# One batched banded-attention kernel: each engine branches on its own, and three loads change their place on SyncE's queue

## The reference

```python
x = x + 0.5 * _L0_ffn_ref(_layernorm(x), gate_w, w1, b1, w2, b2)
x = x + _L0_attn_ref(_layernorm(x), Wq, Wk, Wv, Wo)
x = x + 0.5 * _L0_ffn_ref(_layernorm(x), gate_w, w1, b1, w2, b2)
```

## Time and profile before

| | us |
|---|---|
| median of 3 runs (lowest to highest) | 862.96 (862.14 to 865.73) |
| the profiled execution | 860.79 |
| its span, first to last instruction | 858.7 |
| PE busy in it | 811.9 (95%) |
| DVE, ACT, POOL busy | 743.2, 634.7, 481.3 |
| mean granted TensorE clock | 0.994 of full |

### The profile page before, as it was taken

How to read it: one execution, slowest core, us unless ns; L and a number is a source line. 1 busy time by engine, 2 the same in 40 slices (tenths; PEclk the granted TensorE clock), 3 DMA queues, 4 the chain that set the end, 5 groups by cost and what they waited for, 6 DMA issues and landing times.

```text
span 858.7 us, 50541 instructions
## 1 busy us (share of the span) xinstructions
PE 811.9 (95%) x21504; PEld 611.7 (71%) x21505; DVE 743.2 (87%) x2788; ACT 634.7 (74%) x1418; POOL 481.3 (56%) x856
## 2 busy tenths in 40 slices
PE   9798999999999999999999999899999999999795
PEld 8555666777777777667778778667777777766573
DVE  7898899998987899998888799998988789999663
ACT  2268878997877667898777676899777767788760
POOL 3212556675554566766555466766555465766661
PEclk9999999999999999999999999999999999999899
DMA  7722224332212335442222234533222244321212
GB/s 230 119 83 69 68 77 131 106 106 68 87 52 92 114 105 165 117 123 68 81 74 74 95 126 144 148 103 92 69 71 67 92 126 127 102 75 35 78 43 90
DMA packets 93195, 83.55 MB, mean 97 GB/s; under 512 B 17568, under 2 KB 92192, under 8 KB 92960
## 3 DMA queue, kind: packets, MB, share of 16 engines
q1 hardware_dynamic: 91360, 78.91, 30.3%
q10 hardware_dynamic: 1600, 1.31, 1.0%
HBM read 20.66 MB, written 8.39 MB: 34 GB/s over the span
## 4 chain that ended last, share of the span: by engine, by line
PE 67%; DVE 13%; ACT 9%; issue 4%; SPq 2%; DMA 2%; POOL 1%; ACTq 0%; DVEq 0%
PE bank L1093 14%; PE bank L1075 11%; PE bank L1041 11%; PE bank L930 10%; PE bank L945 6%; PE bank L913 6%; DVE bank L1485 6%; ACT probs L1218 4%; PE bank L1113 3%; PE bank L899 2%; DVE stats L698 1%; SPq L830 1%; ACT xn L1131 1%; PE bank L866 1%; DVE row_max L1485 1%
## 5 line engine op out<-in xcount | busy, mean ns | idle before, releaser
L1218 ACT ACTIVATE probs<-bank 128x384 f32<-128x384 f32 (+1 forms) x1024 | 460.0, 481 | 143.3 <-PE bank L1075 125.2
L1485 DVE CUSTOM_DVE_ANT_0 bank<-bank,con 128x288 f32<-128x288 f32 x1024 | 494.3, 519 | 52.7 <-PE bank L1041 44.4
L1041 PE MATMUL bank<-k_stack,q_stack 96*32 96x288 bf16 x4096 | 325.2, 288 | 9.7 <-DVE row_max L1485 5.1
L1075 PE MATMUL bank<-q_stack,k_stack 99*32 99x288 bf16 (+3 forms) x4096 | 320.3, 286 | 11.4 <-ACT probs L1218 8.3
L1093 PE MATMUL bank<-probs,v_sb 128*32 128x128 f32 x5888 | 307.6, 273 | 6.0 <-issue 4.8
L1287 POOL TENSOR_SCALAR_AFFINE_SELECT probs<-probs 128x512 f32<-128x512 f32 x240 | 154.7, 644 | 179.9 <-ACT probs L1218 179.4
L1093 PEld LDWEIGHTS bank<-probs,v_sb 128*32 128x32 f32 x5888 | 194.2, 111 | 38.4 <-issue 8.2
L1041 PEld LDWEIGHTS bank<-k_stack,q_stack 96*32 96x32 bf16 x4096 | 126.6, 95 | 72.5 <-DVE row_max L1485 21.0
L1075 PEld LDWEIGHTS bank<-q_stack,k_stack 99*32 99x32 bf16 x4096 | 125.2, 95 | 69.2 <-ACT probs L1218 44.3
L1292 POOL TENSOR_SCALAR_AFFINE_SELECT probs<-probs 128x512 f32<-128x512 f32 x240 | 153.6, 640 | 17.0 <-ACT probs L1218 16.9
L930 PE MATMUL bank<-xnT,wqk_sb 128*32 128x256 f32 x2048 | 157.7, 379 | 0.6 <-DVE neg_max L1507 0.5
(11 more groups left out here) (123 smaller groups left out, 718.9 us busy)
## 6 DMA issues: line engine op xcount, KB each, us to landing
q_stack<-pieces SPq DMA_DIRECT2D x384, 64.0 KB, 2.7
k_stack<-pieces SPq DMA_DIRECT2D x364, 64.0 KB, 2.7
x_ring<-in_x SPq DMA_DIRECT2D x28, 512.0 KB, 4.8
out_x<-x_ring SPq DMA_DIRECT2D x16, 512.0 KB, 4.3
attn<-in_x SPq DMA_DIRECT2D x4, 512.0 KB, 6.1
wback_sb<-in_wback SPq DMA_DIRECT2D x8, 256.0 KB, 5.8
k_stack<-pieces ACTq DMA_DIRECT2D x20, 64.0 KB, 3.5
q_stack<-neg_max SPq DMA_DIRECT2D x48, 16.0 KB, 2.3
```

Source lines behind the costliest of these rows:

```text
L1041: last = pe.matmul(a_ring[i % len(a_ring)][SP * s:SP * (s + 1), 0:WIN], q_stack[g % 2][0:KROWS, h, q:q + SP], k_stack[g % 2][0:KROWS, h, q ...
L1075: last = pe.matmul(score_bank(i)[SP * s:SP * (s + 1), start:final], k_stack[g % 2][0:SROWS, h, WINDOW + P * j + SP * s:WINDOW + P * j + SP ...
L1218: act.activation(probs[:, j % 4, h, c0:c1], score_bank(i)[:, c0:c1], ACT.Exp, scale=LOGIT_SCALE).then_inc(S["exp_ready"], 1)
L1485: dve.tensor_tensor_reduce(out=a_ring[i % len(a_ring)][:, 0:WIN], in0=a_ring[i % len(a_ring)][:, 0:WIN], in1=mask, scale=1.0, scalar=con[: ...
```

## The change

In four parts:

1. The first `attend` has no Block any more. Its five functions are called one after the other with the engines, so no barrier stands at its end.
2. Every engine waits for `found` >= 2 (the flag is written), loads the flag into its own register of `kept_flag`, and branches when it gets there. SP, ACT and POOL load it at the end of their streams. PE loads it ahead of the first PROJECT of the last chunk, DVE ahead of that chunk's first PROJECT_IN.
3. The last chunk's store is taken out of SP's stream and stands first in both arms. In the long arm an all-engine barrier follows it.
4. The loads of the last batch's chunks 0 to 2 move to quarters -22, -14 and -6 from the last A, so ahead of MAX of the last group on SP's queue. The fourth stays at 80.

```diff
-        LATE_END = {'LOAD': -22, 'TURN_ATTN': 0, ...
+        LATE_END = {'TURN_ATTN': 0, ...
+        LOADS_AT_END = (-22, -14, -6, 80)
...
-                end(at + plan["LOAD"] if b or phase == "LATE" else -96, "LOAD", i)
+                if phase == "LATE" and b == nb - 1:
+                    end(BATCH * nb + LOADS_AT_END[c], "LOAD", i)
+                else:
+                    end(at + plan["LOAD"] if b or phase == "LATE" else -96, "LOAD", i)
...
-            with nc.Block() as block:
-                @block.sync
-                def _(sp):
+            def load_flag(engine, any_engine):
+                engine.wait_ge(S["found"], 2)
+                for register in kept_flag:
+                    if register.engine == any_engine:
+                        engine.reg_load(register, any_kept[0:1, 0:1])
+            def store(sp, i):
+                for t in range(4):
+                    sp.wait_ge(*emptied("PROJECT", i, t))
+                sp.dma_start(rows(out, i), x_tiles(i)).then_inc(store_of[i][0], 16)
+            last_chunk = late_index[nb - 1, 3]
+            def run_sync(sp):
...
+                            if not (first and i == last_chunk):
+                                store(sp, i)
-                    if not first:
+                    if first:
+                        load_flag(sp, mybir.EngineType.SP)
+                    else:
                         await_stores(sp)
...
                         elif kind == "PROJECT":
                             i, t, k = n
+                            if first and (i, t, k) == (last_chunk, 0, 0):
+                                load_flag(pe, mybir.EngineType.PE)
...
                         elif kind == "PROJECT_IN":
                             i, t = n
+                            if first and (i, t) == (last_chunk, 0):
+                                load_flag(dve, mybir.EngineType.DVE)
...
+            def store_last(sp):
+                store(sp, last_chunk)
             if first:
-                return await_stores, take_left_out
+                run_sync(nc.sync)
+                run_tensor(nc.tensor)
+                run_scalar(nc.scalar)
+                run_gpsimd(nc.gpsimd)
+                run_vector(nc.vector)
+                return store_last, await_stores, take_left_out
...
-        any_expert = nc.values_load(any_kept[0:1, 0:1], min_val=0, max_val=1)
+        kept_flag = nc.alloc_registers("kept_flag", engines=mybir.ALL_ENGINES)
...
+        any_expert = nc.snap(kept_flag, min_val=0, max_val=1)
         with nc.If(any_expert != 0):
+            store_last(nc.sync)
+            nc.all_engine_barrier()
             take_left_out()
...
         with nc.Else():
+            store_last(nc.sync)
             await_stores(nc.sync)
```

More of the change, by code:

```diff
@@ L393, in build @@
         LATE = {'LOAD': -6, 'TURN_ATTN': 1, 'PROJECT': ((7, 8, 10, 10), (12, 12, 14, 14)), 'BASE': 0, 'MOMENTS': (12, 17, 19, 21), 'RSTD': 23, 'STORE': 19}
-        LATE_END = {'LOAD': -22, 'TURN_ATTN': 0, 'PROJECT': ((6, 6, 8, 9), (12, 15, 15, 15)), 'BASE': -2, 'MOMENTS': (12, 16, 16, 23), 'RSTD': 35, 'STORE': 24}
+        LATE_END = {'TURN_ATTN': 0, 'PROJECT': ((6, 6, 8, 9), (12, 15, 15, 15)), 'BASE': -2, 'MOMENTS': (12, 16, 16, 23), 'RSTD': 35, 'STORE': 24}
+        LOADS_AT_END = (-22, -14, -6, 80)
         COUNT_AT = 16
@@ L839, in _, with run_tensor @@
                             i, = n
-                            for t in range(4):
-                                sp.wait_ge(*emptied("PROJECT", i, t))
-                            sp.dma_start(rows(out, i), x_tiles(i)).then_inc(store_of[i][0], 16)
-                    if not first:
+                            if not (first and i == last_chunk):
[3 more added lines that the diff above has]
+                    else:
                         await_stores(sp)
-                @block.tensor
-                def _(pe):
+            def run_tensor(pe):
                     def keep_busy(count):
@@ L1116, in _, with run_scalar @@
                             last.then_inc(full_sem("TURN", n), 1)
-                @block.scalar
-                def _(act):
+            def run_scalar(act):
                     if first:
@@ L1231, in _, with run_gpsimd @@
                             act.activation(o_raw[:, :], o_bank[:, :], ACT.Copy).then_inc(S["o_copied"], 1)
-                @block.gpsimd
-                def _(pool):
+                    if first:
+                        load_flag(act, mybir.EngineType.Activation)
+            def run_gpsimd(pool):
                     for kind, *n in events:
@@ L1309, in _, with run_vector @@
                                 .to_broadcast([P, 4, HG, VW]), ALU.mult).then_inc(S["glob_ready"], 1)
-                @block.vector
-                def _(dve):
+                    if first:
+                        load_flag(pool, mybir.EngineType.Pool)
+            def run_vector(dve):
                     if first:
@@ L1543, in _ @@
                                    .then_inc(S["first_row"], 1)
+            def store_last(sp):
+                store(sp, last_chunk)
             if first:
-                return await_stores, take_left_out
+                run_sync(nc.sync)
[4 more added lines that the diff above has]
+                return store_last, await_stores, take_left_out
+            with nc.Block() as block:
+                block.sync(run_sync)
+                block.tensor(run_tensor)
+                block.scalar(run_scalar)
+                block.gpsimd(run_gpsimd)
+                block.vector(run_vector)
             reset()
-        await_stores, take_left_out = attend(B, x, lambda b: slice(b, b + 1), lambda b, c: slice(NT * b + 4 * c, NT * b + 4 * c + 4), True)
-        any_expert = nc.values_load(any_kept[0:1, 0:1], min_val=0, max_val=1)
+        kept_flag = nc.alloc_registers("kept_flag", engines=mybir.ALL_ENGINES)
+        store_last, await_stores, take_left_out = attend(B, x, lambda b: slice(b, b + 1), lambda b, c: slice(NT * b + 4 * c, NT * b + 4 * c + 4), True)
+        any_expert = nc.snap(kept_flag, min_val=0, max_val=1)
         with nc.If(any_expert != 0):
+            store_last(nc.sync)
+            nc.all_engine_barrier()
             take_left_out()
```

## The result

| | median of the executions, us | against before, 95% interval |
|---|---|---|
| before | 862.96 (862.14 to 865.73) | |
| changed | 854.17 (852.49 to 860.27) | 0.9916 (0.9889 to 0.9944) |
| changed, second set, with a set of before of its own (861.13) | 854.41 (852.80 to 857.93) | 0.9929 (0.9900 to 0.9958) |

What follows compares the result with a forecast made beforehand. PE's in-order stream was taken to bound the kernel. Moved loads 3.9 us plus exit 2.9 us gave 6.8 us, so 856.2 us against the median of 862.96, range 853.9 to 860.2.

Steps and rivals of the forecast that it cites:

- The exit: From last addition to end of span: flag and branch taken per engine, PE's load included, gain 2.9 us.
- PE's load of the flag: Between last transposes and projections: the load takes 1.1 us and makes the projections 0.7 us late.
- SP, a tie by the forecast: At the exit: SP reaches its arm at 851.7, just as the last store's four waits are over.
- DVE's load hidden, no assertion on SP: At the exit: PE's load covers DVE's; an assertion still on SP would move the store's issue from 851.7 to 852.2.
- The stall at 801 is the loads' doing: Drained stage: PE's code fetch stands behind two of three 512 KB loads, leaving PE idle 3.0 us.
- Worth 3.9 us: Drained stage, 800 to 811: removing stall and slow clock gains 3.2 + 0.7 us of ACT's idle time.
- The sum's lower bound of 2.7: Drained stage: the moved loads gain only 2.7 us if ACT's other waits grow to 1 us each.
- What comes in the new place, 0 of 0 to 0.8: Around 781.5 to 786: the moved loads' traffic costs PE 0 to 0.8 us idle, taken as 0.
- the prediction's own signs: Forecast wrong if PE idles over 1.5 us or clock falls in 781 to 790, or DVE's or SP's branch exceeds 4.5.
- The stall moves: Rival, new place of the loads: the code fetch at 780.5 is caught instead, 6.0 us lost; 862.2 us, chance 0.12.
- The loads aren't the cause: Rival, drained stage: the stall at 801 stays and only the exit gains; 860.1 us, chance 0.07.
- The exit doesn't do what it says: Rival, exit: fetches collide with the store's packets or SP arrives late, gain 0.9 not 2.9; 858.2 us, chance 0.12.

Runs made afterwards that it cites:

- `exit_only`: The changed kernel with the last batch's three loads left at quarters 30, 46 and 63; 0.9964 (0.9940 to 0.9988) of before.
- `loads_tiny`: The kernel before with the last batch's loads of chunks 0 to 2 cut to a few bytes; 0.9998 of before, 0.9965 when run again.
- `loads_only`: The kernel before with only the three loads moved, Block and exit as before; 0.9965 (0.9939 to 0.9991) of before.
- `before_again`: The kernel before, unchanged, run for a second profile; its drained stage (420 matmul records) took 16.5 us, against 19.0 in the first.
- `loads_double`: The kernel before with a second load of 512 KB in front of each of the three loads; 0.9991 (0.9970 to 1.0012) of before.
- `loads_spread`: The changed kernel with the three loads each alone between two STACKs of the last group, once the one ahead has landed; 0.9941 (0.9913 to 0.9970) of before.
- `store_in_stream`: The changed kernel with the last store back in SP's own stream, ahead of its load of the flag; 0.9956 (0.9934 to 0.9978) of before.

## Why the prediction was right

- *The exit*, forecast 2.9 us: 3.1 by the time of `exit_only`, and 2.8 to 3.1 by the profiles (7.84 less 4.6 to 4.9, less 0.15 for PE). The sum was right by errors that cancel. PE's load of the flag was put at 1.1 us long and 0.7 on the path; it took 0.49 and cost 0.15 at most: in the chain the gap from the second transposes to the projections is 0.19 us instead of the 0.10 of the earlier trace rows and the transposes are 0.06 longer, and in the profile of `exit_only` nothing at all. The store's landing was put at 2.9 and took 3.7 to 3.9, with instruction packets moving beside it; that they slow it is not shown. DVE came out of its branch after 3.2 to 3.3 us instead of 3.9 and so was not what is late last; the store's landing was. SP, a tie by the forecast, was in its arm in time in the profiles of the changed kernel.
- *DVE's load hidden, no assertion on SP*: right. SP's branch stands 0.1 us behind its load.
- *The stall at 801 is the loads' doing*: right, and shown by `loads_tiny` in the profiles. *Worth 3.9 us*: mis-sized, since the sum was made against one profile, in which the stall and the low clock behind it were the worst of the three that have them; 3.1 in the mean. The sum's lower bound of 2.7 comes out as 2.9 from the two waits of ACT that it names; no end of the range uses it.
- *What comes in the new place, 0 of 0 to 0.8*: this is the step that failed. The prediction looked for a code fetch in the way of the traffic, found 1.5 us to spare, which held in `loads_only` and the changed kernel (no idle piece over 0.6 us), and took "no stack traffic is in the way here". But the last stack DMA was still under way, issued 0.7 us ahead of the first load, and PE waits for it with nothing to spare, as its 0.3 us in before could have told. In two of five profiles it landed after 3.9 instead of 2.4 us and the stretch took 2.7 and 3.2 us longer, with 3.4 us of low clock behind the wait in both. The mean, 1.3 us, stands against the 3.9; the net is 1.8 us by the profiles and 3.0 (0.8 to 5.2) by the time of `loads_only`. With the exit's 3.1 the profiles account for 4.9 of the 6.1 to 7.2 us measured, so that the forecast of 6.8 hit owes something to luck: the loads were put too high by 2.1, and the rest is not accounted for. By the prediction's own signs (idle PE over 1.5 us or a lower clock in the new place) it was wrong in the first profile of the changed kernel, not in the second.
- *The rivals.* "The stall moves" came true in part: not by the fetch at 780.5 but by the stack DMA, and in some executions only. "The loads aren't the cause" falls, and with it, for this burst, the reading that PE gets into its next block of instructions at hardly any cost. "The exit doesn't do what it says" falls.

Open stays why executions of one kernel differ in the opening. Over all profiles record 3000 lies at 148.4 to 154.4 us; the mean of the seven with the new exit is 151.7, that of the seven with the old 150.4. A loss of 1 us in the opening through the change is neither shown nor excluded. The granted clock tells where a part of the scatter arises. In nine profiles a stretch of 3.4 us at 1.2 GHz begins at 26 to 28 us, and record 2400 lies at 128.3 to 129.1 us. In three it begins at 39 us, in the first of before there is none, and the record lies at 126.6 to 127.1. In `before_again` there are three, and it lies at 130.1. Both kinds of kernel are among the nine. So the 1.4 us by which the changed kernel's first profile is behind before's there go with the low clock; of what follows up to record 3000, PE's waits in 126 to 155 name the largest pieces: 1.7 us without a releaser and 1.6 us for ACT, against 0.6 and none in before. Why the stretch comes when it does, no run shows. Open is also which of the two, profile or time, has the worth of `loads_tiny` right.

## What to carry to other kernels

The branch into the other arm cost each engine 2.5 to 5.5 us here; it need not be on the path, if each engine takes it on its own as soon as it has the flag, and what remains to be done is issued from the arm. An idle piece without a releaser, next to a burst of large DMAs on the queues, can be a late code fetch: look for the late packet on the engine's instruction queue, cut the bytes to prove it, and break up or move the burst; but look in the new place for every small transfer that is already under way and has no slack, not only for the next fetch. And make the sum against more than one profile where single executions differ by more than the change.

## What the runs showed of the hardware

- Loading one flag from SBUF took 0.47 to 0.50 us on ACT, PE, SP and POOL when at most three engines did it at a time (the profiles with the new exit), and 1.06 to 1.10 us when all five did it at once behind the barrier. On DVE it took 1.1 to 1.2 us either way.
- The taken branch took PE 3.4 to 3.7 us with the old exit, where the instructions moved after the last store's traffic (3.9 in `loads_double`), and 3.8 to 4.6 us with the new exit, where they moved beside it. Of the others, in the seven profiles with the new exit, POOL took 2.5 to 2.8, DVE 2.9 to 3.7, SP 3.1 to 4.2 and ACT 4.6 to 5.5 us from the branch to the next instruction. The Trainium skill's "Advanced Engine Details and Errata", section "Control Flow Timing", has a compare-and-branch at about 108 ns; the sequencers' own records on the other four are shorter still (45 to 72 ns), and the arrival in the arm 2.5 to 5.5 us later is no part of either figure.
- An idle piece of 2.3 us on PE was not followed by a fall of the granted clock in `before_again`, one of 2.1 us (at 787) in `loads_spread` neither; one of 2.3 us in the first profile of the changed kernel was, for 3.4 us at 1.2 GHz, and so were one of 1.3 us (at 775) in `loads_spread` and one of 1.8 us in `store_in_stream`, for 3.4 us each, and those of 2.7 to 3.6 us, for 3.4 to 6.8. The length of the idle piece alone doesn't decide it.
